# A graph network's edge loops: gathered rows copied into PSUM, with the edge products accumulated on top of them

## The reference

```
# layer 0
msg  = relu(x[src] + edge_attr_64 @ W_e + b_e)
aggr = segment_sum(msg, dst)
h    = silu(bn(((1 + eps) * x + aggr) @ W1 + b1));  h = silu(bn(h @ W2 + b2))
x    = layernorm(x + h)
# layer 1
m    = relu(concat(x[src], edge_attr_128) @ V1.T + b1) @ V2.T + b2
agg  = segment_sum(m, dst)
x    = layernorm(x + x + bn(GRU(agg, x)))
```

## Time and profile before

| | us |
|---|---|
| three executions | 976.2, 978.73, 987.15 |
| their median | 978.73 |
| the profiled execution | 971.74 |
| its span, first to last instruction | 969.9 |
| adds of loop 0, first to last start | 15.89 to 296.76 |
| adds of loop 1, first to last start | 475.13 to 742.27 |

### The profile page before, as it was taken

One profiled execution on the slowest core, in us unless ns is written; L12 is line 12 of the kernel. 1 busy time (PEld: TensorE's weight loads), 2 busy tenths in 40 slices (PEclk: granted clock), 3 DMA queues, 4 the chain that ended last, 5 costly groups with the idle time before them and its releaser, 6 DMA issues.

```text
span 969.9 us, 11501 instructions
## 1 busy us (share of the span) xinstructions
PE 814.6 (84%) x3686; PEld 618.6 (64%) x3686; DVE 758.9 (78%) x1326; ACT 367.3 (38%) x597; POOL 396.6 (41%) x381
## 2 busy tenths in 40 slices
PE   4977777777777999979688878888888999999993
PEld 2534444444445999968456656666665789899893
DVE  5899999999997992458789999999998535435255
ACT  2444544554454441321245544555554221111122
POOL 3466666666660100011577767767772000000001
PEclk9999999999998999979889999999999999999997
DMA  8678777767780004003666667677663011010011
GB/s 281 216 246 232 203 207 204 202 202 206 206 266 17 1 1 174 1 2 127 204 193 199 201 200 217 199 213 207 207 196 112 9 65 67 1 66 1 1 44 63
DMA packets 50758, 137.21 MB, mean 141 GB/s; under 512 B 8256, under 2 KB 8512, under 8 KB 50311
## 3 DMA queue, kind: packets, MB, share of 16 engines
q0 software_dynamic: 26720, 87.58, 31.0%
q1 hardware_dynamic: 23974, 48.86, 15.4%
HBM read 128.67 MB, written 7.74 MB: 141 GB/s over the span
## 4 chain that ended last, share of the span: by engine, by line
PE 41%; DVE 39%; issue 13%; DMA 2%; ACT 1%; POOL 1%; DVEq 1%; SPq 0%; POOLq 0%; ACTq 0%
PE banks L486 33%; DVE raw L1030 14%; DVE msg_lo L1018 13%; PE banks L510 4%; DVE hot L1010 3%; DVE attr_lo L949 2%; DVE agg L1044 2%; DMA raw<-xb_dram,src_sb 2%; DVE attr_hl L949 1%; PE banks L525 1%; DVE stats L1158 1%; PE banks L526 1%; PE banks L562 1%; DVEq L1034 1%; DVE last L1318 1%
## 5 line engine op out<-in xcount | busy, mean ns | idle before, releaser
L819 ACT ACTIVATE msg_hi<-raw 128x512 fp32r<-128x512 f32 x334 | 211.1, 632 | 282.5 <-DVE raw L1030 188.5
L1030 DVE TENSOR_TENSOR raw<-banks,raw 128x512 f32<-128x512 f32 x334 | 227.3, 681 | 18.7 <-PE banks L510 11.8
L1018 DVE SCALAR_TENSOR_TENSOR msg_lo<-raw,msg_hi 128x512 fp32r<-128x512 f32 x334 | 227.1, 681 | 0.1
L415 POOL DMA_INDIRECT raw<-table_dram,src_sb x167 | 193.4, 1158 | 81.3 <-issue 60.2
L525 PE MATMUL banks<-msg_hi,hot 128*128 128x512 f32 x334 | 153.8, 461 | 80.4 <-DVE msg_lo L1018 65.8
L415 POOL DMA_INDIRECT raw<-xb_dram,src_sb x155 | 163.3, 1053 | 93.0 <-DVE msg_lo L1018 47.4
L525 PEld LDWEIGHTS banks<-msg_hi,hot 128*128 128x128 f32 x334 | 63.1, 189 | 168.4 <-DVE msg_lo L1018 123.4
L437 POOL TENSOR_TENSOR moments<-moments,minus_half 128x1 f32<-128x1 f32 x32 | 20.4, 636 | 317.2 <-DVE moments L1164 317.2
L526 PE MATMUL banks<-msg_lo,hot 128*128 128x512 f32 x334 | 132.8, 398 | 0.0
L510 PE MATMUL banks<-V1e_hi,attr_hi 128*128 128x512 f32 x167 | 70.4, 422 | 7.5 <-DVE attr_lo L949 7.5
L510 PE MATMUL banks<-We_hi,attr_hl 128*128 128x512 f32 x167 | 69.4, 416 | 8.4 <-DVE attr_hl L949 8.4
(11 more groups left out here) (159 smaller groups left out, 1440.2 us busy)
## 6 DMA issues: line engine op xcount, KB each, us to landing
attr_sb<-in_attr SPq DMA_DIRECT2D x84, 128.0 KB
attr_sb<-in_attr SPq DMA_DIRECT2D x42, 256.0 KB
Wg_raw<-in_Wg SPq DMA_DIRECT2D x3, 1536.0 KB, 6.4
W_raw<-in_W SPq DMA_DIRECT2D x2, 2048.0 KB
raw<-table_dram,src_sb POOLq DMA_INDIRECT x167
x_in<-in_x SPq DMA_DIRECT2D x5, 512.0 KB, 12.6
xb_dram<-xb SPq DMA_DIRECT2D x5, 512.0 KB, 4.2
rows<-in_x SPq DMA_DIRECT2D x1, 2560.0 KB, 13.0
```

Of the source, the lines that this page charges most:

```text
L415: pool.indirect_dma_start(raw[L][:, t % RAW, :], None, table, bass.IndirectOffsetOnAxis(ap=src_sb[:, t:t + 1], axis=0)).then_inc(gathered[ ...
L819: nc.scalar.activation(msg_hi[L][:, a:a + len(tiles), :], raw[L][:, b:b + len(tiles), :], ACT.Relu).then_inc(relued[L], 1)
L1018: nc.vector.scalar_tensor_tensor(msg_lo[L][:, a:a + len(tiles), :], raw[L][:, b:b + len(tiles), :], 0.0, msg_hi[L][:, a:a + len(tiles), :] ...
L1030: nc.vector.tensor_tensor(rows, banks[:, a:a + len(tiles), :], rows, ALU.add).then_inc(added[L], 1)
```

## The change

The gathered rows are copied into PSUM, and TensorE adds the edge product to them there. In detail:

- `add_products` is gone. A copy `place` moves the gathered row block of an even tile by VectorE and of an odd tile by ScalarE from `raw` into one of five banks (0 to 3 and 6). It waits for the gather and for the low part of the tile five before, which had that bank.
- The products of `edge_product` go into that bank without the flag that starts a new sum, so they add to what the copy left there. They wait for the copy. `prime` lets TensorE write all five banks once with a starting matmul ahead of each loop; the first copies wait for it.
- relu (high part) and low part read the bank and no longer `raw`. The slot of `raw` is free once it is copied: a gather waits for the copy of the tile eight before.
- All engines go by steps of two tiles. The order within a step changes on VectorE (low parts of the two tiles before, then the copy of tile 2j+2, then every second step attributes and one-hots) and on ScalarE (relu of tiles 2j-1 and 2j, the copy of tile 2j+3, then every second step the attributes' high part). SUM_LAG is two steps. One piece of xb is made in a step, not in a tile.
- Bank 6 being taken, a window's turned sums go back into the sum bank from which they came, and a window's first sum waits for the window addition two windows before (`window_added`). x is turned into banks 5 and 7.
- `msg_hi` and `msg_lo` get six slots each, in place of four.

The diff, cut to its core (buffers, the leftover loop, helpers and blank lines left out):

```
...
-JOIN = 1
-UNITS = -(-TILES // JOIN)
+STEPS = -(-TILES // 2)
-RAW, EDGE_BANKS, MSG, HOT, RING = 8, 4, 4, 3, 3
-LOW_LAG, SUM_LAG = 2 // JOIN, 4 // JOIN
+RAW, PLACE_BANKS, MSG, HOT, RING = 8, 5, 6, 3, 3
+SUM_LAG = 2
-COPY_AFTER, TURN_AFTER, ADD_AFTER = 0, 1, 2
+COPY_AFTER, TURN_AFTER, ADD_AFTER = 0, 1, 1
...
-        turn_bank, degree_bank = bank[6], bank[7]
+        place_bank = [bank[0], bank[1], bank[2], bank[3], bank[6]]
+        degree_bank = bank[7]
+        start_bank = [bank[5], bank[7]]
...
@@ -411,7 +421,8 @@
                 else:
                     wait_table(L)
-                wait(pool, low[L], -(-(t - RAW + 1) // JOIN))
+                if t >= RAW:
+                    pool.wait_ge((placed_odd if odd(t) else placed_even)[L], (t - RAW) // 2 + 1)
                 pool.indirect_dma_start(raw[L][:, t % RAW, :], None, table,
                                         bass.IndirectOffsetOnAxis(ap=src_sb[:, t:t + 1], axis=0)
                                         ).then_inc(gathered[L][t % RAW], 16)
...
-            def edge_product(L, u):
-                wait(pe, added[L], u - EDGE_BANKS // JOIN + 1)
-                for t in unit_tiles(u):
-                    c, ks = t // CHUNK, slice(t % CHUNK * P, (t % CHUNK + 1) * P)
-                    if t % CHUNK == 0:
-                        pe.wait_ge(attr_split[L], c + 1)
-                    acc = bank[t % EDGE_BANKS]
-                    if L == 0:
-                        passes = [(attr_hl[:, c % RING, ks], We_hi[:, :]), (attr_hl[:, c % RING, ks], We_lo[:, :])]
-                    else:
-                        hi, lo = attr_hi[:, c % RING, ks], attr_lo[:, c % RING, ks]
-                        passes = [(hi, V1e_hi[:, :]), (hi, V1e_lo[:, :]), (lo, V1e_hi[:, :])]
-                    if L == 0 and t < FROM_X:
-                        if t == 0:
-                            pe.wait_ge(be_split, 1)
-                        passes += [(ones_row[:, :], be_hi[:, :]), (ones_row[:, :], be_lo[:, :])]
-                    for n, (features, W) in enumerate(passes):
-                        mm = nc.tensor.matmul(acc, features, W, start=n == 0, stop=n == len(passes) - 1)
+            def edge_product(L, t):
+                i, c, ks = t // 2, t // CHUNK, slice(t % CHUNK * P, (t % CHUNK + 1) * P)
+                if t % CHUNK == 0:
+                    pe.wait_ge(attr_split[L], c + 1)
+                pe.wait_ge((placed_odd if odd(t) else placed_even)[L], i + 1)
+                if L == 0:
+                    passes = [(attr_hl[:, c % RING, ks], We_hi[:, :]), (attr_hl[:, c % RING, ks], We_lo[:, :])]
+                else:
+                    hi, lo = attr_hi[:, c % RING, ks], attr_lo[:, c % RING, ks]
+                    passes = [(hi, V1e_hi[:, :]), (hi, V1e_lo[:, :]), (lo, V1e_hi[:, :])]
+                if L == 0 and t < FROM_X:
+                    passes += [(ones_row[:, :], be_hi[:, :]), (ones_row[:, :], be_lo[:, :])]
+                for n, (features, W) in enumerate(passes):
+                    mm = nc.tensor.matmul(edge_bank(t), features, W, start=False, stop=n == len(passes) - 1,
+                                          skip_group_check=True)
                 mm.then_inc(add_mm[L], 1)
...
+            def prime(L):
+                pe.wait_ge((be_split, vb2_split)[L], 1)
+                for b in place_bank:
+                    mm = nc.tensor.matmul(b, ones_row[:, :], (be_hi, v_b2_hl)[L][0:1, :], start=True, stop=True)
+                mm.then_inc(primed[L], 1)
+            def sum_product(L, t):
+                g, c = t // GROUP, t // CHUNK
+                start, stop = t % GROUP == 0, t % GROUP == GROUP - 1 or t == TILES - 1
+                pe.wait_ge(low[L], t + 1)
+                if t % CHUNK == 0:
+                    pe.wait_ge(hot_ready[L], c + 1)
+                if start:
+                    wait(pe, window_added[L], g - 1)
+                    if L == 0 and g == 1:
+                        pe.wait_ge(agg_start, BLOCKS)
...
-                for u in range(UNITS + SUM_LAG + TURN_AFTER):
-                    if u < UNITS:
-                        edge_product(L, u)
-                    if L == 0:
-                        for b in range(u * JOIN, min(BLOCKS, (u + 1) * JOIN)):
-                            turn_x(b)
-                    if L == 0 and u == 12:
+                prime(L)
+                for j in range(STEPS + SUM_LAG + TURN_AFTER):
+                    if j < STEPS:
+                        for t in step_tiles(j):
+                            edge_product(L, t)
+                            if L == 0 and t < BLOCKS:
+                                turn_x(t)
+                    if L == 0 and j == 8:
                         pe.wait_ge(left_ready, 1)
+                        pe.wait_ge(agg_start, BLOCKS)
                         nc.tensor.matmul(misc[0:1, 16:17], left_n[:, 0:1], ones[:, 0:1], start=True,
                                          stop=True).then_inc(left_counted, 1)
-                    if 0 <= u - SUM_LAG < UNITS:
-                        sum_product(L, u - SUM_LAG)
+                    if 0 <= j - SUM_LAG < STEPS:
+                        for t in step_tiles(j - SUM_LAG):
+                            sum_product(L, t)
                     for g in range(GROUPS):
-                        if last_unit(g) + SUM_LAG + TURN_AFTER == u:
+                        if last_step(g) + SUM_LAG + TURN_AFTER == j:
                             turn_window(L, g)
...
-                tiles = unit_tiles(u)
-                act.wait_ge(added[L], u + 1)
-                wait(act, summed[L], u - MSG // JOIN + 1)
-                a, b = tiles.start % MSG, tiles.start % RAW
-                nc.scalar.activation(msg_hi[L][:, a:a + len(tiles), :], raw[L][:, b:b + len(tiles), :],
-                                     ACT.Relu).then_inc(relued[L], 1)
+            def place(L, t):
+                wait_gathered(act, L, t)
+                if t < PLACE_BANKS:
+                    act.wait_ge(primed[L], 1)
+                else:
+                    act.wait_ge(low[L], t - PLACE_BANKS + 1)
+                copy(edge_bank(t), raw[L][:, t % RAW, :]).then_inc(placed_odd[L], 1)
+            def message_high(L, t):
+                act.wait_ge(add_mm[L], t + 1)
+                wait(act, summed[L], t - MSG + 1)
+                nc.scalar.activation(msg_hi[L][:, t % MSG, :], edge_bank(t), ACT.Relu).then_inc(relued[L], 1)
             def start_sums(b):
...
                 for c in range(2):
                     high_features(L, c)
+                place(L, 1)
                 chunk = 2
-                for u in range(UNITS + SUM_LAG + COPY_AFTER):
-                    while chunk < min(CHUNKS, chunks_in(u + 1) + 1):
+                for j in range(STEPS + SUM_LAG + COPY_AFTER):
+                    if 0 < j <= STEPS and 2 * j - 1 < TILES:
+                        message_high(L, 2 * j - 1)
+                    if 2 * j < TILES:
+                        message_high(L, 2 * j)
+                    if 2 * j + 3 < TILES:
+                        place(L, 2 * j + 3)
+                    if L == 0:
+                        for b in step_tiles(j):
+                            if b < BLOCKS:
+                                start_sums(b)
+                    while chunk < min(CHUNKS, chunks_in(j + 1) + 1):
                         high_features(L, chunk)
                         chunk += 1
-                    if L == 0:
-                        for b in range(u * JOIN, min(BLOCKS, (u + 1) * JOIN)):
-                            start_sums(b)
-                    if u < UNITS:
-                        message_high(L, u)
                     for g in range(GROUPS):
-                        if last_unit(g) + SUM_LAG + COPY_AFTER == u:
+                        if last_step(g) + SUM_LAG + COPY_AFTER == j:
                             copy_window(L, g)
...
-            def low_messages(L, u):
-                tiles = unit_tiles(u)
-                dve.wait_ge(relued[L], u + 1)
-                a, b = tiles.start % MSG, tiles.start % RAW
-                nc.vector.scalar_tensor_tensor(msg_lo[L][:, a:a + len(tiles), :], raw[L][:, b:b + len(tiles), :], 0.0,
-                                               msg_hi[L][:, a:a + len(tiles), :].bitcast(F32), ALU.max,
+            def low_message(L, t):
+                dve.wait_ge(relued[L], t + 1)
+                nc.vector.scalar_tensor_tensor(msg_lo[L][:, t % MSG, :], edge_bank(t), 0.0,
+                                               msg_hi[L][:, t % MSG, :].bitcast(F32), ALU.max,
                                                ALU.subtract).then_inc(low[L], 1)
-            def add_products(L, u):
-                tiles = unit_tiles(u)
-                for t in tiles:
-                    wait_gathered(dve, L, t)
-                dve.wait_ge(add_mm[L], u + 1)
-                a, b = tiles.start % EDGE_BANKS, tiles.start % RAW
-                rows = raw[L][:, b:b + len(tiles), :]
```

(41 more changed lines are left out.)

88 lines of the change are left out of this document (41 added, 47 removed).

## The result

The changed kernel took 989.11 us (median of 20 runs, 985.5 to 996.57), the kernel before beside it 978.16 us (974.33 to 987.15): a ratio of 1.0113, 95% interval 1.0089 to 1.0137. It is slower by 1.1%; 954 us had been predicted. The profiled execution took 988.19 us (span 986.4), the one before 971.74 (969.9).

What follows compares the result with a forecast made beforehand. VectorE was taken to bound the old kernel, a new ring of waits the changed one. Loop 0 gains 16.5 us less 3, loop 1 11.4, together 25: from the runs' median 978.73 to 954 us, range 930 to 981.

Steps and rivals of the forecast that it cites:

- The ring: Both loops: once-per-chunk cycle of waits (copy, product, relu, ScalarE copy, high part, split, low parts), 5.81 and 5.79 us.
- copy and hand-over: First piece of the ring: VectorE's copy into PSUM and its hand-over to TensorE, 0.69 + 0.06 = 0.75 us.
- split and one-hots: Piece of the ring on VectorE: attribute split and one-hots, 1.45 us in loop 0, 1.20 in loop 1.
- the window chunk: One chunk in three: the window addition lengthens the ring by 0.60 us in loop 0, 0.80 in loop 1.
- fast and slow copies: Two rivals on copies into PSUM: at the cast's rate, 932 us (10%); slow, gain eaten, up to 1004 us (17%).
- GpSimd was no bound: Rival: GpSimd's gathers, one a chunk held to the full, bound both loops at 6.15 us a chunk, 963 us; 8%.
- a low part with an operand in PSUM cannot hold a gather: Both loops: with one PSUM operand, VectorE's low part does not delay gathers, so GpSimd stays under the ring, at 954 us.
- The two starts: Beginnings of the loops: 3 us charged to loop 0 because xb is finished later, at about 39 us; 0 for loop 1.
- TensorE is granted its 2.4 GHz level: Edge loops: clock at 9 tenths or more in nearly all slices of the kernel before, so full clock was assumed.
- the hand-over from TensorE: Piece of the ring: product plus 0.04 us until ScalarE starts its relu, 0.77 us in loop 0, 1.00 in loop 1.
- those 2.6 us: Quiet stretch of loop 1, kernel before: VectorE idle 2.6 us over 145 tiles; VectorE taken as the bound.
- The chances: Forecast 60%, fast copy 10%, GpSimd 8%, slow copies 17%, loose ring 5%; stated as faster 0.73, same 0.15, slower 0.12.

Runs made afterwards that it cites:

- e1: Changed kernel with VectorE taking the low half of a chunk's edge attributes one step (two tiles) later; 909.43 us, 0.9334 of the kernel before.
- c1: Control: the changed kernel unchanged except for a blank line, run again; 957.07 us, 0.9857 of the kernel before, no late signal.
- c2: Control: the kernel before, run again for its trace beside the changed kernel's on one chip; 969.95 us, no late signal.
- e2: Changed kernel with xb made at two blocks a step instead of one; 950.2 us, 0.9763 of the kernel before.
- e3: Changed kernel with 8 extra unread matmuls of 256 columns per chunk in TensorE's idle gap, loop 0 only; 954.74 us, 0.9791 of the kernel before.
- e13: Changed kernel with 3 extra matmuls of 512 columns per chunk in TensorE's idle gap, loop 0 from tile 24; 954.25 us, 0.9824 of the kernel before.
- e5: Changed kernel with VectorE's attribute split one step later and xb at two blocks a step; 902.6 us, 0.931 of the kernel before; 999.3 with late signals.
- e7: Changed kernel with split one step later, xb at two blocks a step, all row copies on ScalarE; 993.83 us, 1.023 of the kernel before; 882.1 without late signals.
- e10: The e3 kernel once more, in a series with late signals; 987.33 us, 1.0136 of the kernel before.
- e11: The e5 kernel once more, in a series with late signals; 999.33 us, 1.0259 of the kernel before.
- series 2 and 6: Series 2: c1, c2 and e5, without late signals (957.07, 969.95, 902.6 us). Series 6: e10 and e11, with them (987.33, 999.33 us).
- series 7: Runs of the changed kernel with extra matmuls in TensorE's gap: 3 of 512 columns (954.25 us) or 24 of 32 (985.84 us); no late signals.
- series 4 and 6: Series with late signals. Series 4: changed kernel again (980.7 us), e6 (990.08), e7 (993.83). Series 6: e10 (987.33), e11 (999.33).
- e6: Changed kernel with VectorE copying the odd tiles' rows too and ScalarE none; 990.08 us, 1.0151 of the kernel before, with late signals.

## Why the prediction was wrong

**The ring: right.** It was derived from waits that did not yet exist, and held to 0.03 us in loop 0. Part of that is luck: copy and hand-over took 0.83 us for 0.75, split and one-hots 1.35 for 1.45 (of the 1.45, 0.12 is a delay between a low part and the split behind it, 203.86 to 204.58 in place of 0.60; behind a wait it does not arise). In loop 1, where split and one-hots took 1.22 for 1.20, the copy's 0.08 stays: the ring is that much too short (5.87 for 5.79), and so is the window chunk (6.68 for 6.59); with 18.42 us for three chunks against 18.84 before, loop 1 gains 0.035 us a tile, not 0.072. e1 shows by taking one link out that it is this ring that bound the loops.

**The copies, the rivals and the gathers.** 0.68 and 0.60 us lie in the predicted range; fast and slow copies both fall. GpSimd was no bound. By the rule of the Trainium skill, page "SBUF — State Buffer", section "Who interferes with whom", a low part with an operand in PSUM cannot hold a gather; the trace agrees, with 959 in place of 1058 ns.

**The two starts.** The charge of 3 us for loop 0 was too small: c1's low part of tile 12 comes 6.6 us after c2's (59.64 and 53.09), and e2 gives 4.9 of them back. I had the last addition for xb at 39 us; it began at 42.2.

**"TensorE is granted its 2.4 GHz level".** Read from a kernel in which TensorE never waited long, and wrong for this one, whose matmuls come in bursts with a gap of 1.9 us behind them in each chunk (c1). In the sum it is a small error, 2 to 3 us in loop 0 (e3, e13).

**What turned the sign: the hand-over from TensorE.** This is the step that failed. The ring has the product "with 0.04 to ScalarE [...] 0.77 and 1.00" for each of 84 chunks. In c1 no signal is late. There the sum reads: loop 0 ends 11.0 us earlier than in c2 (289.54 against 300.53; predicted 13.5), the stretch to loop 1 takes 1.4 more, loop 1 4.5 less (257.97 against 262.49; predicted 11.4) and the rest 0.4 more: 13.7 gained, span 954.4 against 968.1. That is a result of the predicted kind at half its size. In the first trace the hand-over fails, and at each of the seven places above it costs 1.5 us or more. Against c1 loop 0 ends 13.5 us later and loop 1 takes 19.2 us more; with -0.7 between and behind them this is the whole difference of the spans, 986.4 against 954.4. The kernel before lost 2.8 us so in loop 1 (223.4 against 220.5 from tile 24) and nothing in loop 0.

It could have been seen. In the trace of before, in the chunk of tile 52 of loop 1 (timeline):

```profile
565.53 0.40 PE L510 MATMUL banks<-V1e_hi,attr_lo 128*128 128x512 f32 x1
...
569.29 0.69 DVE L1030 TENSOR_TENSOR raw<-banks,raw 128x512 f32<-128x512 f32 x1 [2.18 <-PE banks L510]
570.01 0.63 ACT L819 ACTIVATE msg_hi<-raw 128x512 fp32r<-128x512 f32 x1 [2.31 <-PE banks L526]
```

This add is that of tile 56, and tile 56's product was over at 565.93: the signal came at 569.193, over 3 us late, where a product is otherwise ready 1.8 us before its add. The stretch of the earlier trace rows contains it, and 2.18 of the 2.6 us that VectorE waited for TensorE there are this one place; 0.38 us before the add at 666.37 are a second one. I took those 2.6 us for nothing. No term of the sum and no rival had a TensorE that answers late.

The chances, too, were added up wrongly: as the text splits them they give 0.77, 0.15 and 0.09 for faster, same and slower, not 0.73, 0.15 and 0.12.

**What stays open.** Late signals are no property of this change alone: with them e5 loses 94 to 97 us, e7 112, the changed kernel 24 to 34, the kernel before some 5 (means of the table). For one kernel the long chunks sit mostly at the same tiles, they are more where tiles follow each other faster, and neither the idle gap nor transposes just before decide them, as e10 and e11 show. Whether chip, machine or hour brings them is not settled: series 2 and 6 had the same chip number and differed. Whether the faster kernels suffer through TensorE's work or through the number of its instructions could not be tried, since series 7 met none.

One thing in the traces divides the two surroundings without exception. The thirteen traces without late signals hold 11183 to 11203 records of semaphore updates each; the six of the first measurement and of series 4 and 6 that are full of them hold 5819 to 6880, and the first trace of the kernel before, which has few, holds 8132. The same kernel has the same number of instructions in both. What is missing is missing in the edge loops: from 100 to 150 us the changed kernel's first trace has 290 such records and c1's 1004. So where signals were late, the trace also lost records of them. Every execution on record has its granted clock noted, so none is known to have run without recording, and the obvious rival, that the recording itself delays the signals and that the sign of the first result is its doing, is untested. The Trainium skill, page "NOTIFIC — the notification-queue block", section "7.1 Overflow: three behaviours, one of which stalls the engine", says that the block which writes out the engines' records can, in one of its modes, stall the engine when a queue is full. That would fit, but no run here shows such a stall. All that is shown is the signature, its price, and that it comes together with lost records.

## What to carry to other kernels

Before predicting a kernel that will lean on another engine's answers, go through the single long waits of the old trace, not only the mean of a group: 2.18 us before one add of 145 was the chief warning of 32. When experiments on a changed kernel all come out well below it, repeat the unchanged one before explaining any of them, and repeat it in more than one series: here the sign of the change differs between series (0.984 to 0.986, or 1.006 to 1.011). Compare the number of semaphore records in the traces as well: a trace that has lost half of them is a warning about its times. A ring of waits is worth breaking at the link that has slack to spare: issuing one VectorE instruction two tiles later took 957 us to 909, with xb made earlier to 903, and with all copies on ScalarE to 882, all of them below both kernels where no signals are late, but each of these last two is slower than both (999 and 994) where late signals occur.

## What was unexpected of the hardware

TensorE's completion signals can be 2 to 5 us late, once 9 (e6: product over at 516.74, relu at 526.00), and then arrive 42 to 51 ns apart, in traces that have also lost a quarter to a half of their semaphore records. The granted clock falls after such a pause (at 221.1, 262.1, 579.5 and 678.5 us in the changed kernel). A low clock is not needed for it: in the chunk of tile 132 the clock was at its upper level from 251.8 to 262.1 us, and the product begun at 255.87 was answered 3.8 us late. And half clock for 34 to 38 us of a loop costs 2 to 3 us when other engines set the pace.
